# A three-layer graph network on one core: each layer opens with three blocks of plain tiles and closes with three blocks of edge tiles

## The reference

```python
for l in range(W.shape[0]):            # 3 layers
    h = x @ W[l].T
    agg = segment_sum(h[src] * norm[:, None], dst) + b[l]
    mean = agg.mean(0); var = ((agg - mean) ** 2).mean(0)
    x = relu(gamma[l] * (agg - mean) * rsqrt(var + BN_EPS) + beta[l])
x = layernorm(x_in + x)
x = layernorm(x + edge_network(x, src, dst, ...))
```

## Time and profile before

| | us |
|---|---|
| median of three runs | 1739.05 (1737.77 to 1739.99) |
| the profiled execution, its own time | 1743.42 |
| its span in the trace | 1741.7 |
| layer 0, first matmul of block 0 to first of layer 1 | 196.3 to 555.0 |
| layer 1 | 555.0 to 865.3 |
| layer 2 | 865.3 to 1136.5 |
| PE busy over the span | 1375.5 (79%) |
| DVE, ACT, POOL busy | 1205.7, 948.3, 975.6 |

### The profile page before, as it was taken

One profiled execution on the slowest core, in us unless ns is written; L12 is line 12 of the kernel. 1 busy time (PEld: TensorE's weight loads), 2 busy tenths in 40 slices (PEclk: granted clock), 3 DMA queues, 4 the chain that ended last, 5 costly groups with the idle time before them and its releaser, 6 DMA issues. The chain is left out here.

```text
span 1741.7 us, 27484 instructions
## 1 busy us (share of the span) xinstructions
PE 1375.5 (79%) x8020; PEld 1179.2 (68%) x8020; DVE 1205.7 (69%) x3400; ACT 948.3 (54%) x1906; POOL 975.6 (56%) x986
## 2 busy tenths in 40 slices
PE   4676699999989799999979999935454179999633
PEld 3555488888877688888768888824444068888622
DVE  7247466566665676768667778848777379999765
ACT  3462244334425677767466666428777534444576
POOL 5770667777773687877443333206777644344146
PEclk8589699999999999999989999957566589999955
DMA  2000887878777577777555566279998433323112
GB/s 61 1 2 3 259 301 263 270 256 272 247 239 275 184 253 247 255 255 247 201 185 191 199 210 213 103 227 379 412 398 358 184 92 88 94 84 92 35 75 110
DMA packets 130924, 340.37 MB, mean 195 GB/s; under 512 B 34972, under 2 KB 67220, under 8 KB 127990
## 3 DMA queue, kind: packets, MB, share of 16 engines
q1 hardware_dynamic: 74486, 175.45, 28.6%
q0 software_dynamic: 56320, 163.51, 27.9%
HBM read 166.40 MB, written 177.40 MB: 197 GB/s over the span
## 5 line engine op out<-in xcount | busy, mean ns | idle before, releaser
L1020 PE MATMUL ps_b<-yhi,whi 128*128 128x492 f32 (+1 forms) x960 | 397.1, 414 | 18.9 <-ACT aggT L912 14.3
L1020 PE MATMUL ps_b<-ylo,whi 128*128 128x492 f32 (+1 forms) x960 | 378.2, 394 | 0.0
L1020 PE MATMUL ps_b<-yhi,wlo 128*128 128x492 f32 (+1 forms) x960 | 377.8, 394 | 0.0
L912 ACT COPY aggT<-ps_b 128x492 f32<-128x492 f32 (+1 forms) x240 | 137.6, 574 | 319.8 <-PE ps_b L1020 319.7
L830 DVE BATCH_NORM_STATS2 stat<-aggT 128x6 f32<-128x492 f32 (+1 forms) x240 | 161.9, 676 | 145.6 <-ACT aggT L912 145.4
L672 POOL DMA_INDIRECT rows<-rows_out,node_at x160 | 180.8, 1130 | 110.4 <-ACT rows_out L918 63.3
L1020 PEld LDWEIGHTS ps_b<-yhi,whi 128*128 128x128 f32 x960 | 185.6, 193 | 50.2 <-ACT aggT L912 14.7
L1020 PEld LDWEIGHTS ps_b<-yhi,wlo 128*128 128x128 f32 x960 | 184.0, 192 | 38.1
L1020 PEld LDWEIGHTS ps_b<-ylo,whi 128*128 128x128 f32 x960 | 185.2, 193 | 30.2 <-issue 0.5
L679 POOL TENSOR_TENSOR X<-X,own_row 128x1016 f32<-128x1016 f32 x40 | 96.4, 2412 | 131.5 <-ACT X L896 131.3
L1253 PE MATMUL fin_ps_x<-ident,fin_X 128*123 128x128 f32 (+1 forms) x320 | 69.8, 386 | 102.8 <-DVE fin_xr L1178 73.9
(11 more groups left out here) (345 smaller groups left out, 3223.5 us busy)
## 6 DMA issues: line engine op xcount, KB each, us to landing
z<-aggT SPq DMA_DIRECT2D x30, 1016.0 KB, 5.1
z<-aggT SPq DMA_DIRECT2D x30, 984.0 KB, 6.1
x_rows<-R SPq DMA_DIRECT2D x80, 256.0 KB, 3.6
fin_xr<-x_rows SPq DMA_DIRECT2D x20, 1024.0 KB, 8.1
X<-z SPq DMA_DIRECT2D x20, 1016.0 KB, 8.1
X<-z SPq DMA_DIRECT2D x20, 984.0 KB, 7.6
fin_X<-z SPq DMA_DIRECT2D x10, 1016.0 KB, 12.6
fin_X<-z SPq DMA_DIRECT2D x10, 984.0 KB, 13.2
```

The lines of the kernel that those rows point to most:

```text
L912: nc.scalar.copy(f.aggT[t % 2][:, j, 0:cols(t)], f.ps_b[j % 2][:, 0:cols(t)]).then_inc(x["copied"], 1)
L1020: o = nc.tensor.matmul(f.ps_b[j % 2][:, 0:n], w[:, c, j * P:(j + 1) * P], y[g % 2][:, c, 0:n], start=(c == 0 and i == 0), stop=(c == C - 1 ...
```

## The change

`kinds` becomes `PPP`, seven times `EP`, then `EEE`: edge blocks are 3, 5, ..., 15, 17, 18, 19. `FB` is the first edge block, now 3. In layers 1 and 2 its shift, source and merge stay in turn 1, and its join and low move to turn 2, where those of other edge blocks would be too. The special code that put join and low into turn 1 no longer fires.

```diff
-        self.kinds = "PP" + "EP" * (self.NE - 2) + "EE"
+        self.kinds = "PPP" + "EP" * (self.NE - 3) + "EEE"
...
+    FB = m.kinds.index("E")
...
                 if late:
                     for j in range(4):
-                        shift(layer, 2, j)
-                elif m.edges(t + 1):
+                        shift(layer, FB, j)
+                if m.edges(t + 1) and not (late and t + 1 == FB):
                     for c in range(C):
                         join(layer, t + 1, c)
...
-                    if m.edges(t + 1) and j in (1, 2) and not late:
+                    if m.edges(t + 1) and j in (1, 2) and not (late and t + 1 == FB):
                         low(layer, t + 1, 2 * j - 2)
                         low(layer, t + 1, 2 * j - 1)
-                    if layer > 0 and m.edges(t + 3) and t >= 0:
+                    if layer > 0 and m.edges(t + 3) and t + 3 > FB:
                         shift(layer, t + 3, j)
...
-                    if m.edges(t + 2) and not (layer > 0 and t == 0):
+                    if m.edges(t + 2) and not (layer > 0 and t + 2 == FB):
                         merge(layer, t + 2, j)
                     if late and j in (1, 2):
-                        merge(layer, 2, 2 * j - 2)
-                        merge(layer, 2, 2 * j - 1)
-                    if late and j == 2:
+                        merge(layer, FB, 2 * j - 2)
+                        merge(layer, FB, 2 * j - 1)
+                    if late and j == 2 and t + 1 == FB:
                         for c in range(C):
                             join(layer, 2, c)
...
                 if late:
                     for j in range(4):
-                        source(layer, 2, j)
+                        source(layer, FB, j)
```

More of the change, by code:

```diff
@@ L975, in body @@
                     if m.edges(t + 1):
-                        for c in ((), (), (), range(C))[j] if late else (range(0, 2), range(2, 4), (), ())[j]:
+                        for c in ((), (), (), range(C))[j] if late and t + 1 == FB else (range(0, 2), range(2, 4), (), ())[j]:
                             high(layer, t + 1, c)
-                    if layer > 0 and m.edges(t + 3):
+                    if layer > 0 and m.edges(t + 3) and t + 3 > FB:
                         source(layer, t + 3, j)
```

## The result

The kernel before took 1739.99 us (median of 5, 1737.77 to 1746.13), the changed kernel 1758.17 (1751.14 to 1764.74): ratio 1.0105, 95% interval 1.0068 to 1.0141. The forecast of 1730 us and its range of 1719 to 1740 were wrong, and so was the sign.

What follows compares the result with a forecast made beforehand. PE, busy 79% of the span, was taken to bound layers 1 and 2, POOL's chain of issues layer 0. -6.4 - 2.2 + 1 - 4.0 + 2.6 = -9.0 us took the median 1739.05 to 1730, range 1719 to 1740.

Steps and rivals of the forecast that it cites:

- What is next to be late is the join of block 3: Layer 1, turn 2: edge-data scatters push back POOL's weigh of block 3; +1 us, bounds 0 and 2.2.
- POOL's writes of rows hold the weigh back from the join: nothing: Layer 1's close: PE comes later than the carries and row writes keep the weigh off the join; no cost.
- The first stall stays: Turn 1, layers 1 and 2: PE's 7.23 and 7.10 us wait for ACT's copy of block 1 remains; ACT's reordering costs nothing.
- rival B: Layers 1 and 2: block 4's smaller load pieces let the fourth gather land in time, saving 7.2 + 7.1 us: 1716; chance 0.1.
- The second stall goes: Layers 1 and 2: the wait for block 2's low part disappears, -2.2 us in layer 1, -4.0 in layer 2.
- Layer 0: -6.4 forecast: Layer 0's start: fewer POOL issues before turn 1, so block 18's own rows start at 469.1 instead of 475.52.
- 1.48 each: Layer 0: POOL's steady time per issue, 144 in 213.6 us, waits included, taken from the kernel before.
- rival C: Layer 0 gives nothing: block 3's place waits behind tables, or 16-issue turns run slower; 1736.5 us, chance 0.28.
- The close in layer 2: +2.6 forecast: Layer 2, turns 16 and 17: DVE's extra work and weighs on joins delay PE's merges; +2.6 us, bounds 0 and 9.2.
- Rival D: Layers 1 and 2, turn 16: block 19's last gather lands late, costing PE 7.2 us each: 1744.5; chance 0.12.

Runs made afterwards that it cites:

- the first trace: Profiled execution of the changed kernel, the slowest of its five: 1764.74 us, layer 1 328.7 us.
- the second trace: Changed kernel, unchanged, run again on another chip: median 1945.1 us, ratio 1.008 to the kernel before; layer 1 329.8 us.
- the kernel with the scatters moved: Changed kernel with the forty edge-data scatters moved from layer 1 to layer 2: 1936.9 us, ratio 1.0005 to the kernel before; layer 1 306.2 us.
- four in flight: Changed kernel with four instead of two semaphores, so a scatter waits for the one four before: 1928.6 us, ratio 1.0028; layer 1 310.0 us.
- The two holds: Block 4's load held until DVE's first shifts: changed kernel with scatters in layer 2, weigh held, 1729.4 us (.9931); kernel before, 1928.2 us (.9965).
- The tables run: Changed kernel, scatters in layer 2, weigh held, layer 0's two big tables loaded in turns 0 and 3, not -1 and 0: 1733.0 us, .9964.
- group 3: Four kernels on one chip, all with scatters in layer 2 and weigh held, ratios .9925 to .9993; the kernel before took 1740.6 us there.
- both obstacles gone: Changed kernel with scatters in layer 2 and weigh held until the previous edge block's joins: .9968, again 1.0001, with layer 0's tables later .9964.
- with the load held: Changed kernel with scatters in layer 2, weigh held, and block 4's load sent only after DVE shifted block 3: 1729.4 us, ratio .9931.
- the old close as well: Three plain blocks opening, two edge blocks closing, scatters in layer 2, weigh held, block 4's load held: 1915.8 us, ratio .9889 to the kernel before.

## Why the prediction was wrong

**The step that failed: "What is next to be late is the join of block 3 ... I put +1 us on it (bounds 0 and the 2.2 just gained)."** The queue was right, POOL with the weigh behind the scatters; the size and the length of it were not. In place of +1 us the late weighs cost 16 us in turns 3 to 14 of layer 1, and 6 more in turn 16. The join of block 3 itself cost PE nothing in the first trace (turn 2: 12.5 us) and 4.4 us in the second (16.9). The prediction names the wait of each scatter for the one two before, but puts no price on it, and it bounds the loss by one turn's gain. Two things were missed. The wait is long: right behind the gathers it took 5.42 us (6.05 in the second trace), as much as four issues. And POOL has no slack to pay it back: a pair of turns took POOL 31 to 33 us while the waits lasted, and PE 28.9 undisturbed. So the delay did not end with turn 2: each pair of turns added a landing wait of its own, and PE paid in turns 4, 8, 12 and 14 (15 us over the turns of the kernel with the scatters moved). That it hangs on the scatters is shown by moving them, and that it is the wait for the landing by putting four in flight.

**"In layer 1 ... POOL's writes of rows hold the weigh back from the join: nothing."** The writes did hold the weigh back, and that was the harm: the join needs it. Turn 16 cost 6.3 us. With the scatters gone it costs nothing (16.1), so this too hangs on POOL being late.

**"The first stall stays ... I cost this at nothing."** Wrong in our favour: 4.61 and 4.86 us instead of 7.23 and 7.10. The load of block 4, now in smaller pieces, lets the gather through sooner: 9.1 and 9.5 us to DVE against 11.1 and 10.8. This is rival B's mechanism at a third of its price. The two holds show in both orders that this load makes the gather late, most plainly in layer 2; that the pieces are what differs follows from the ranges above and was not tried by itself, and in layer 1 one trace of the new opening still had 11.1. The rule of the Trainium skill (DMA: Bandwidth & Descriptors, Queues, rings and completion order), that an engine goes round its queues packet by packet, bears on this: the trace now agrees in direction, since the gather is sooner beside smaller pieces, and no run here tells packets apart.

**"The second stall goes":** right, in both layers, as far as DVE's low part goes (in the second trace another wait, for the weigh, took its place in layer 1), and layer 2's turn 2 is at clock 1.00. The opening of layer 2 gained more than 4.0: turns 1 and 2 of layer 2 took 32.9 us, 7.5 over undisturbed turns, where before it was 14.1 over the earlier trace rows.

**Layer 0: -6.4 forecast, +3.9 measured.** POOL's timeline, own rows of blocks 0, 3, 5, 17, 18 and 19:

```profile
178.52 1.05 POOL L668 DMA_INDIRECT R<-in_x,node_at  x1 [46.80 <-DVE R L858]
205.43 1.01 POOL L668 DMA_INDIRECT R<-in_x,node_at  x1 [5.71 <-DMA node_at<-others,free_row]
235.05 1.03 POOL L668 DMA_INDIRECT R<-in_x,node_at  x1 [0.30 <-issue]
452.43 1.03 POOL L668 DMA_INDIRECT R<-in_x,node_at  x1 [1.10 <-DMA node_at<-others,free_row]
479.45 1.03 POOL L668 DMA_INDIRECT R<-in_x,node_at  x1 [3.50 <-issue]
503.82 1.03 POOL L668 DMA_INDIRECT R<-in_x,node_at  x1 [1.19 <-DMA node_at<-others,free_row]
```

The wait for places was 5.71 and not 3.11; block 5 came at 235.05 (forecast 230.6), block 17 at 452.43 (444.2), block 18 at 479.45 (469.1). The step that failed is the steady rate, "1.48 each" taken over from the kernel before: from block 5 to block 17 the same 144 issues took 217.4 us instead of 213.6, and 27.0 instead of 24.9 for the next 16. The tables run shows that a quicker start is given back. That is rival C's second ground, issues that run slower than before. How much layer 0 loses is not settled: the kernel before took 358.7 us, the same layer 0 code in group 3 took 361.6, and changed orders with that start took 361.8 to 365.0; within groups the changed orders lie between 10 us below and 12 above the old one.

**The close in layer 2: +2.6 forecast, about +5 measured.** Turns 15 to 17 took 49.4 us, 6.2 over three undisturbed ones at 14.4; before, turn 17 was 0.6 over. It lies inside the bounds (0 to 9.2). The joins and PE's two waits:

```profile
1103.10 6.87 DVE L775 TENSOR_TENSOR X<-X,V 128x508 f32<-128x508 f32 x4
...
1121.96 6.85 DVE L775 TENSOR_TENSOR X<-X,V 128x508 f32<-128x508 f32 x4
```
```profile
1112.44 2.04 PE L1009 MATMUL ps_m<-sel,G 128*128 128x128 f32 x8 [1.94 <-DVE carry L764]
1130.70 1.13 PE L1009 MATMUL ps_m<-sel,R 128*128 128x128 f32 x8 [1.83 <-DVE carry L764]
```

The mechanism was right (6.8 us forecast for the first join); the second join, for which I counted 1 us more, cost the full 4.4, and turn 16's clock fell to 0.91. The second trace of the changed kernel and the one with four in flight have 16.6 and 20.8 us for turns 16 and 17, 2.6 us more in sum, with PE waits of 1.94 and 3.37 us on the same carries.

**Rival D**, the last gather, was not seen: PE's waits in turns 16 and 17 are all on carries.

## What to carry to other kernels

When a block moves, look at every queue it drags along: the third plain block was harmless to PE, but it put four scatters right behind the gathers, where one waited 5.42 us for a landing. Before bounding a delay by one turn, compare that engine's time per period with the bound's: without slack the delay is not made good, and each period adds its own. And when an order loses, test the same order with the obstacle gone and the old order with the same edit. Here the same order with both obstacles gone came to between 0 and -0.4%, and with the load held to -0.7%; -1.1% took the old close as well, and the hold gives 0.35% to the old order too.

## What the runs showed of the hardware that I had not expected

- A gather of the same size took 10.1 to 11.5 us from issue to use with a load of one large piece per lane behind it, 8.9 to 10.2 in layer 2 (7.1 to 11.1 in layer 1) with a load in four pieces, and 6.4 to 7.0 with none.
- A scatter right behind gathers held the one two later for 5.42 and 6.05 us (changed kernel, two traces); with four in flight none waited.
- The kernel before took 1740 us in two of five measurements, each group on a chip of its own, and 1924 to 1938 us in the three others, 11% more: layers 1 and 2 are nearly equal, while the start, layer 0 and the part after the layers are longer. No run here tells why. Only the traces of the longer kind have turns of layer 1 that are up to 6 us too long without a wait for another engine; these are unexplained.
- The granted clock of turn 16 of layer 2 was 0.91 with a PE wait of 1.94 us in it, 1.00 in another trace of the same kernel with the same wait, and 1.00 with 1.2 us of idle PE when the weigh was held.
